# A graph kernel with 6,656 gathers: each gather waits until GpSimd is done with the one ahead

## The chip, the cores and the metric

The kernel runs on one core of one Trainium2 chip. The metric is the device time of one execution in microseconds; the number given for a kernel is the median of its runs.

## What is computed

Two layers of a graph network over 6,250 nodes of 128 features and 206,250 edges (200,000 drawn at random and a loop per node). The first weighs, sums and feeds a small network; the second makes three hops of attention over the edges. Cut to its core:

```python
def _L0_gnn_ref(x, edge_index, edge_weight, W1, b1, W2, b2):
    msg = edge_weight[:, None] * x[src]
    agg = jax.ops.segment_sum(msg, dst, num_segments=N)
    h = jax.nn.relu((x + agg) @ W1 + b1)
    return h @ W2 + b2

def _L1_gnn_ref(entity_emb, edge_emb, q_w, k_w, edge_index, edge_type, ...):
    rel = edge_emb[edge_type]
    for _ in range(3):
        h, t = agg[head], agg[tail]
        att = jnp.sum((h @ q_w) * jnp.tanh(rel * t @ k_w), axis=1)
        w = segment_softmax(att, head)
        agg = segment_sum(w[:, None] * rel * t, head) / max(count, 1)
        agg = agg / norm(agg)
        out = out + agg + entity_emb
    return out

x = _layernorm(x + _L0_gnn_ref(...))
x = _layernorm(x + _L1_gnn_ref(...))
```

What matters here is `x[src]` in the first layer and `agg[tail]` in each hop: a row of 512 bytes, found by an index, for every edge, four times over.

## The kernel before

Edges are sorted by the node that they end in (first layer) or start from (hops), so that each section of 128 nodes owns a run of tiles of 128 edges. There are 1,664 tiles (`slot_tiles`), worked on in 416 groups of four (`GROUP`). The program has four long stages that go over all 416 groups: the first layer, with the second sort woven into it, and hops 0, 1 and 2. Short stages lie ahead, between and behind.

In each long stage one gather fetches the 128 node rows of one tile, one row to a partition. It is an indirect DMA of GpSimd, which alone can issue one: GpSimd makes the descriptors and starts the transfer. `pool_rows` (L616) issues them. A batch is two groups (`BATCH`), eight gathers. The gathered rows go to a ring of four groups (`RING`), two batches; the indices to a buffer of two batches. For a batch GpSimd waits until the rows of the ring are consumed (`s_free`, which is `s_rt`) and until ScalarE has copied the indices (`s_copy_idx`), and then issues eight gathers without any wait between them. Each gather adds 16 to `sp_tail` of its group when its data have landed. The first two batches of a stage are written out, all others are in a loop whose waits are against registers (`freed`, `copied`).

In a hop the others do this with a group, each lagging behind the last by a few groups. SyncE loads the group's type rows (`rel`), its mask and four windows of `qt`. VectorE multiplies the type rows with the gathered rows (`rt<-banks,tails`, L1771) once they have landed, and signals `s_rt`. TensorE turns the product (L1833), multiplies it with `k_sb` (L1829); ScalarE copies (`rtt`, L1853) and takes the tanh (`right`, L1849). TensorE makes the attention (L1818), VectorE its minimum (L1759), ScalarE the exponentials (`weight`, L1866), TensorE turns those (L1825) and sums the tile into its section (L1838), and VectorE adds that to the accumulator (L1753). ScalarE copies a batch's indices with `idx<-tails_of_slots` (`scalar_idx`, L645 to L650; the first two batches in `first_idx`, L641) once `s_rt` says that the indices of the batch before were used. So the loop is: gathers, landing, product on VectorE, index copy on ScalarE, the wait of GpSimd, gathers.

In the first layer VectorE and TensorE do a lighter job of the same shape, and ScalarE weighs the gathered rows (L1394) and signals `s_rt`.

Of the kernel before, what the change touches and what calls it, by code (L numbers as in the profile page):

```python
# [145 lines left out]
def phases(e, name, step, groups, total, rates, unroll=UNROLL):  # L146

    regs = {rate: e.alloc_register(f"{name}_rate{rate}") for rate in rates}
    spare = [e.alloc_register(f"{name}_until{n}") for n in range(8)]
    for start in range(0, total, IN_BLOCK):  # L150
        whole = start + IN_BLOCK <= total
        for i in range(start, start + 2 * unroll if whole else total):
            step(Step(e, i, groups))
        if whole:
            turns = IN_BLOCK // unroll - 2
            for rate in rates:
                e.reg_mov(regs[rate], rate)
            with e.Fori(0, turns) as turn:
                for b in range(unroll):
                    step(Step(e, start + 2 * unroll + b, groups, turn, regs, spare, unroll, turns))  # L160
                for rate in rates:
                    e.reg_add(regs[rate], regs[rate], rate)
    for r in [*regs.values(), *spare]:
        e.free_register(r)


def gnn_two_layers(nc, x, src, dst, edge_type, edge_weight, w1, b1, w2, b2, edge_emb, q_w, k_w, out):
    z = Sizes(x.shape[0], src.shape[0], x.shape[1], edge_emb.shape[0])
    assert z.D == P and z.T * 2 == P and z.groups % UNROLL == 0
    top = ExitStack()  # L170
    with top:
        def sem(name):
            return Sem(top.enter_context(nc.semaphore(name)))

        def tensor(ctx, name, shape, dt=F32):
            return ctx.enter_context(nc.sbuf_tensor(name, shape, dt))
# [25 lines left out]
        s_iota, s_consts = sem("s_iota"), sem("s_consts")  # L202
# [404 lines left out]
        sums = acc_of[:, :, 0:z.D]  # L607
        sp_tail = [sem(f"sp_tail{i}") for i in range(RING)]
        s_copy_idx, s_taken, s_acc, s_rt = sem("s_copy_idx"), sem("s_taken"), sem("s_acc"), sem("s_rt")
        stretches = range(0, z.slot_tiles, BANK)  # L610
        full, odd_rows = divmod(z.N, P)

# [2 lines left out]

        def pool_rows(e, name, rows, idx, of, s_free):  # L616

            def batch(b):
                for t in range(BATCH * GROUP):
                    g = b * BATCH + t // GROUP  # L620
                    e.indirect_dma_start(out=rows[:, g, t % GROUP, :], out_offset=None, in_=of,  # L621
                                         in_offset=bass.IndirectOffsetOnAxis(ap=idx[:, b, t:t + 1], axis=0)).then_inc(sp_tail[g].h, 16)

            for b in range(2):
                e.wait_ge(s_copy_idx.h, s_copy_idx.at(b + 1))
                batch(b)
            freed, copied = e.alloc_register(f"freed_{name}"), e.alloc_register(f"copied_{name}")
            e.reg_mov(freed, s_free.at(BATCH))
            e.reg_mov(copied, s_copy_idx.at(3))
            with e.Fori(0, z.slot_groups // BATCH // 2 - 1):  # L630
                for b in range(2):
                    e.wait_ge(s_free.h, s_free.at(BATCH))
                    e.wait_ge(s_free.h, freed)
                    e.wait_ge(s_copy_idx.h, copied)
                    batch(b)
                    e.reg_add(freed, freed, BATCH)
                    e.reg_add(copied, copied, 1)
            e.free_register(freed)
            e.free_register(copied)

        def first_idx(e, others, idx):  # L641
            for b in range(2):
# [21 lines left out]
        with ExitStack() as ctx:  # L664
# [359 lines left out]
            begun = tensor(ctx, "runs_begun", [H, K, P])  # L1024
# [3 lines left out]
            idx = tensor(inner, "l0_idx", [P, 2, BATCH * GROUP], I32)  # L1028
# [385 lines left out]
            with nc.Block() as block:  # L1414
# [24 lines left out]
                def _(e):  # L1439
                    phases(e, "gt", tensor_l0, z.slot_groups, steps, (UNROLL, GROUP * UNROLL))  # L1440
            inner.close()
            s_copy_idx.base += z.slot_groups // BATCH + 1
            for s in (s_rt, s_acc):
                s.base += z.slot_groups
# [251 lines left out]
        for hop in range(HOPS):  # L1696
            with ExitStack() as ctx:
                qt = tensor(ctx, f"qt{hop}", [P, z.NP])
                idx = tensor(ctx, f"idx{hop}", [P, 2, BATCH * GROUP], I32)
# [242 lines left out]
                def scalar_nodes(e):  # L1942
                    a, b = squares
                    e.wait_ge(s_taken.h, s_taken.at(z.slot_tiles))
                    e.activation(square[:, a:b, :], sums[:, a:b, :], ACT.Square).then_inc(s_root.h, 1)
                    e.activation(square[:, b:, :], sums[:, b:, :], ACT.Square).then_inc(s_root.h, 1)
                    e.wait_ge(s_node.h, s_node.at(10))
                    e.activation(norm[:, :], norm[:, :], ACT.Sqrt).then_inc(s_root.h, 1)
# [3 lines left out]
                with nc.Block() as block:  # L1952
                    @block.sync
                    def _(e):
                        e.wait_ge(s_qt.h, s_qt.at(node_groups))
                        pipeline(e, f"hs{hop}", sync_hop, z.slot_groups, deep, (UNROLL,) if first else (UNROLL, GROUP * UNROLL))
                        if first:
                            for s in s_keep:
                                e.wait_ge(s.h, 32 * z.slot_groups // UNROLL)
                        if hop < HOPS - 1:  # L1960
                            for n, (a, b) in enumerate(zip(thirds, thirds[1:])):
                                e.wait_ge(s_node.h, s_node.at(13 + n))
                                e.dma_start(node_rows.rearrange("(t p) d -> p t d", p=P)[:, a:b, :], agg[:, a:b, :]).then_inc(s_next.h, 16)
                            e.wait_ge(s_next.h, 48 * (hop + 1))

                    @block.gpsimd
                    def _(e):
                        pool_rows(e, f"hop{hop}", tails, idx, node_rows, s_rt)

                    @block.vector  # L1970
                    def _(e):
                        vector_q(e)
                        pipeline(e, f"hd{hop}", vector_hop, z.slot_groups, deep, (UNROLL, 2 * UNROLL, GROUP * UNROLL, 16 * GROUP, 32))
                        vector_nodes(e)

                    @block.tensor
                    def _(e):
                        tensor_q(e)
                        pipeline(e, f"he{hop}", tensor_hop, z.slot_groups, deep, (UNROLL, GROUP * UNROLL, 16 * GROUP))

                    @block.scalar
                    def _(e):
                        first_idx(e, others, idx)
                        scalar_q(e)
                        pipeline(e, f"ha{hop}", scalar_hop, z.slot_groups, deep, (UNROLL, GROUP * UNROLL, 32))
                        scalar_nodes(e)
                s_copy_idx.base += z.slot_groups // BATCH + 1
                for s in (s_oht, s_rel, s_copied) if first else (s_copied,):
                    s.base += z.slot_groups
# [60 lines left out]
```

## Time and profile before

| | us |
|---|---|
| median of three runs | 9158.42 |
| lowest, highest | 9154.59, 9167.25 |
| span of the profiled execution | 14895.7 |
| GpSimd busy in it | 6417.6 |
| TensorE busy in it (matmuls) | 9009.4 |
| VectorE, ScalarE busy in it | 6224.1, 6149.7 |

The profiled execution's own time is known by its span alone. It is 5,737 us longer than the median of the runs that were timed without a profiler. Busy times and counts of instructions are those of the program; waits and idle times are those of the profiled execution, and have to be weighed one by one. The gathers are the rows of line L621. A gather's record covers GpSimd's work on it, not the transfer.

### The profile page before, as it was taken

The numbers are of one execution on the slowest core, as the hardware profiler recorded it, in microseconds if no ns is written. First come the engines' busy times: TensorE is split into PE (matmuls) and PEld (weight loads), VectorE is DVE, ScalarE is ACT, GpSimd is POOL, SyncE is SP. The second block draws the span as 40 slices with busy tenths as digits, with TensorE's granted clock in tenths as the row PEclk, the third lists the DMA queues.
The fourth block names the chain that finished last, engine by engine and source line by source line (L and its number), as shares of the span: only waits on it lengthen the run. The fifth ranks groups of instructions, "written<-read, shape, count | busy, mean of one in ns | idle before, by whom it ended". The sixth has DMA issues, their size and how long they took to land. (4 is left out here: it accounts for less than half of the span.)

```text
span 14895.7 us, 251017 instructions
## 1 busy us (share of the span) xinstructions
PE 9009.4 (60%) x47197; PEld 6806.5 (46%) x47197; DVE 6224.1 (42%) x27880; ACT 6149.7 (41%) x15788; POOL 6417.6 (43%) x6756
## 2 busy tenths in 40 slices
PE   2465555566777777777755555555555556555665
PEld 2343443444555555555544444444444444444444
DVE  3555555565333333333343333333334333333334
ACT  1355555553333333333334444444443444444443
POOL 4554554442444434444334444444434444444443
PEclk7566666667777777777777777777777777777777
DMA  2111111112444444444433333333343333333333
GB/s 63 37 37 34 36 35 35 33 35 77 127 125 126 125 125 126 125 125 126 124 102 105 106 104 106 104 105 101 108 99 105 104 104 107 102 105 105 109 109 93
DMA packets 1390477, 1399.81 MB, mean 94 GB/s; under 512 B 239512, under 2 KB 1066681, under 8 KB 1390137
## 3 DMA queue, kind: packets, MB, share of 16 engines
q1 hardware_dynamic: 1173398, 951.42, 21.2%
q0 software_dynamic: 216064, 444.28, 12.3%
q10 hardware_dynamic: 876, 2.56, 0.1%
q8 instruction: 51, 0.84, 0.0%
q14 instruction: 88, 0.71, 0.0%
HBM read 888.87 MB, written 183.76 MB: 72 GB/s over the span
## 5 line engine op out<-in xcount | busy, mean ns | idle before, releaser
L621 POOL DMA_INDIRECT tails<-node_rows,idx x4992 | 4732.3, 948 | 6564.6 <-ACT idx L649 5017.2
L1753 DVE SCALAR_TENSOR_TENSOR acc<-acc,fade,banks 128x129 f32 x4992 | 1718.4, 344 | 5486.8 <-remote 3164.9
L1838 PE MATMUL banks<-rt,weight_t 128*128 128x129 f32 x9984 | 1783.3, 335 | 1486.3 <-issue 802.1
L1838 PEld LDWEIGHTS banks<-rt,weight_t 128*128 128x128 f32 x9984 | 1607.8, 244 | 1631.4 <-issue 1206.6
L621 POOL DMA_INDIRECT l_rows<-in_x_dram,l_idx x1664 | 1585.1, 953 | 1529.5 <-ACT l_idx L649 1017.3
L1846 ACT ACTIVATE weight_t<-banks 128x512 f32<-128x512 f32 x1248 | 745.5, 597 | 3569.1 <-remote 2286.4
L1825 PE MATMUL banks<-ident,weight 128*128 128x128 f32 x4992 | 1070.4, 353 | 1878.0 <-ACT weight L1866 1767.1
L1818 PE MATMUL banks<-right,window 128*128 128x128 f32 x9984 | 1774.8, 335 | 459.9 <-issue 459.2
L1818 PEld LDWEIGHTS banks<-right,window 128*128 128x128 f32 x9984 | 1590.2, 242 | 538.2 <-issue 510.7
L1829 PE MATMUL banks<-rtt,k_sb 128*128 128x512 f32 x2496 | 1741.3, 789 | 1.4 <-ACT rtt L1853 1.4
L1825 PEld LDWEIGHTS banks<-ident,weight 128*128 128x128 f32 x4992 | 752.0, 181 | 2041.5 <-ACT weight L1866 1931.4
L1759 DVE CUSTOM_DVE_ANT_0 att<-banks,mask 128x128 f32<-128x128 f32 x4992 | 1236.7, 285 | 888.7 <-remote 574.4
L1866 ACT ACTIVATE weight<-att,low 128x128 f32<-128x128 f32 x4992 | 1583.4, 395 | 1.7 <-DVE low L1789 1.5
L1853 ACT ACTIVATE rtt<-banks 128x512 f32<-128x512 f32 x1248 | 743.4, 596 | 1597.2 <-remote 1447.3
L1849 ACT ACTIVATE right<-banks 128x512 f32<-128x512 f32 x1248 | 744.4, 596 | 1535.2 <-remote 798.3
L1833 PEld LDWEIGHTS banks<-ident,rt 128*128 128x128 f32 x4992 | 781.9, 172 | 1247.7 <-issue 894.1
L1771 DVE TENSOR_TENSOR rt<-banks,tails 128x512 f32<-128x512 f32 x1248 | 857.9, 687 | 547.2 <-remote 180.2
L1833 PE MATMUL banks<-ident,rt 128*128 128x128 f32 x4992 | 937.3, 321 | 241.5 <-DVE rt L1771 237.0
L1239 ACT ACTIVATE apart<-spread,spot_left 128x256 f32<-128x256 f32 x1534 | 655.2, 495 | 1030.0 <-remote 761.9
L1406 PE MATMUL banks<-l_weighed,l_hot 128*128 128x128 f32 x3328 | 756.5, 395 | 428.2 <-DVE acc L1371 217.7
L1406 PEld LDWEIGHTS banks<-l_weighed,l_hot 128*128 128x128 f32 x3328 | 649.6, 289 | 559.2 <-issue 549.1
L1394 ACT ACTIVATE l_weighed<-l_rows,l_weights 128x128 f32<-128x128 f32 x1664 | 526.8, 387 | 546.1 <-remote 394.4
(309 smaller groups left out, 9792.2 us busy)
## 6 DMA issues: line engine op xcount, KB each, us to landing
window<-qt SPq DMA_DIRECT2D x4992, 64.0 KB
rel<-rel_kept SPq DMA_DIRECT2D x832, 256.0 KB
rows_in<-tile_rows SPq DMA_DIRECT2D x416, 256.0 KB
rel_kept<-rel SPq DMA_DIRECT2D x416, 256.0 KB
mask<-mask_kept SPq DMA_DIRECT2D x832, 128.0 KB
tails<-node_rows,idx POOLq DMA_INDIRECT x4992
mask_kept<-mask SPq DMA_DIRECT2D x416, 128.0 KB
l_rows<-in_x_dram,l_idx POOLq DMA_INDIRECT x1664
```

Source lines behind the costliest of these rows:

```text
L621: e.indirect_dma_start(out=rows[:, g, t % GROUP, :], out_offset=None, in_=of, in_offset=bass.IndirectOffsetOnAxis(ap=idx[:, b, t:t + 1], a ...
L1406: mm = s.e.matmul(bank[g2][:, t * P:t * P + P], hot[:, g2, t, :], weighed[:, g2, t, :], start=True, stop=True)
L1753: e.scalar_tensor_tensor(to, to, fade[:, g2, t:t + 1], bank[b_acc + t // 2][:, t % 2 * WIDE:t % 2 * WIDE + WIDE], ALU.mult, ALU.add).then_ ...
L1759: e.tensor_tensor_reduce(att[:, g2, t, :], bank[b_att][:, t * P:t * P + P], mask[:, g4, t, :], 1.0, START, ALU.add, ALU.min, tile_low[:, g ...
L1771: e.tensor_tensor(rt[:, g4, :, 0:z.D], of, tails[:, g8, :, :], ALU.mult).then_inc(s_rt.h, 1)
L1818: mm = e.matmul(bank[b_att][:, t * P:t * P + P], window[:, g4, t, :], right[:, g2, t * P:t * P + P], start=True, stop=True)
L1825: mm = e.transpose(bank[b_et][:, t * P:t * P + P], weight[:, g2, t, :], ident[:, :])
L1829: e.matmul(bank[b_kw][:, :], k_sb[:, :], rtt[:, s.slot(2, 2), :], start=True, stop=True).then_inc(s_kw.h, 1)
L1833: mm = e.transpose(bank[b_rtt][:, t * P:t * P + P], rt[:, s.slot(1, UNROLL), t, 0:z.D], ident[:, :])
L1838: mm = e.matmul(bank[b_acc + t // 2][:, t % 2 * WIDE:t % 2 * WIDE + WIDE], weight_t[:, s.slot(4, 2), t, :], rt[:, s.slot(4, UNROLL), t, :] ...
L1846: e.activation(weight_t[:, s.slot(4, 2), :, :].rearrange("p t d -> p (t d)"), bank[b_et][:, :], ACT.Copy).then_inc(s_ets.h, 1)
L1866: e.activation(weight[:, g2, t, :], att[:, g2, t, :], ACT.Exp, scale=-1.0, bias=low[:, g4, t + 1:t + 2]).then_inc(s_exp.h, 1)
```

## The change

A semaphore (`s_iota`, used at the start of the program up to the value 2 and free since) counts the gathers that GpSimd has finished: each gather gets `engine_sem=s_begun.h`, by which GpSimd adds one when its own work on the gather is done, which is not when the data have landed. A register `begun` counts how many have been issued. Each gather but the first of a batch waits until the semaphore has reached the register, that is until the gather ahead is done. The wait against a constant above it is always met by then. At the end of each stage the base of the semaphore moves on by 1,664.

```diff
         s_copy_idx, s_taken, s_acc, s_rt = sem("s_copy_idx"), sem("s_taken"), sem("s_acc"), sem("s_rt")
+        s_begun = s_iota
+        s_begun.base += 2
...
         def pool_rows(e, name, rows, idx, of, s_free):
+
+            begun = e.alloc_register(f"begun_{name}")
+            e.reg_mov(begun, s_begun.at(0))
 
             def batch(b):
                 for t in range(BATCH * GROUP):
                     g = b * BATCH + t // GROUP
+                    if t:
+                        e.wait_ge(s_begun.h, s_begun.at(1))
+                        e.wait_ge(s_begun.h, begun)
                     e.indirect_dma_start(out=rows[:, g, t % GROUP, :], out_offset=None, in_=of,
-                                         in_offset=bass.IndirectOffsetOnAxis(ap=idx[:, b, t:t + 1], axis=0)).then_inc(sp_tail[g].h, 16)
+                                         in_offset=bass.IndirectOffsetOnAxis(ap=idx[:, b, t:t + 1], axis=0), engine_sem=s_begun.h)\
+                        .then_inc(sp_tail[g].h, 16)
+                    e.reg_add(begun, begun, 1)
...
-            e.free_register(freed)
-            e.free_register(copied)
+            for r in (freed, copied, begun):
+                e.free_register(r)
...
             s_copy_idx.base += z.slot_groups // BATCH + 1
+            s_begun.base += z.slot_tiles
...
```

The order of the other engines' instructions is the same before and after. On GpSimd, the end of hop 0's written-out batches and its loop before:

```order
L621 DMA tails<-node_rows,idx 128x128 x16
L630 UNCONDITIONAL_BRANCH
L621 DMA tails<-node_rows,idx 128x128 x8
L636 ISA
L621 DMA tails<-node_rows,idx 128x128 x8
L636 ISA
L630 COMPARE_AND_BRANCH
```

And the second batch of that loop now, with the semaphores that a row waits for (`s_iota` is the one that counts finished gathers):

```order
L629 DMA tails<-node_rows,idx 128x128 [waits s_copy_idx,s_rt]
L632 REGISTER_ALU
L629 DMA tails<-node_rows,idx 128x128 [waits s_iota]
L632 REGISTER_ALU
L629 DMA tails<-node_rows,idx 128x128 [waits s_iota]
L632 REGISTER_ALU
L629 DMA tails<-node_rows,idx 128x128 [waits s_iota]
```

Eight gathers that followed each other with nothing between now have a register instruction behind each (the last one's is merged with those that end the batch) and a wait ahead of each but the first. The wait against the register is an instruction of its own in the built program, and the one against the constant is carried by the gather.

## Rows read from the trace of the kernel before

**Rows 1.** The page: span, and part 1, busy us of each engine
```profile
span 14895.7 us, 251017 instructions
PE 9009.4 (60%) x47197; PEld 6806.5 (46%) x47197; DVE 6224.1 (42%) x27880; ACT 6149.7 (41%) x15788; POOL 6417.6 (43%) x6756
```

**Rows 2.** Line L621: durations min/median/max ns; what ended idle time: us, times
```profile
L621 POOL DMA_INDIRECT tails<-node_rows,idx x4992: 939/946/1395, 3532.0 to 14810.8; - x200
L621 POOL DMA_INDIRECT l_rows<-in_x_dram,l_idx x1664: 939/946/1212, 160.5 to 3251.3; - x185
...
  ACT idx L649: 5017.2, 618
  issue: 1900.0, 5891
```

**Rows 3.** Timeline of POOL, one batch in hop 1: start us, us, what, idle
```profile
9009.08 0.96 POOL L621 DMA_INDIRECT tails<-node_rows,idx  x1 [7.24 <-ACT idx L649]
...
9017.84 0.94 POOL L621 DMA_INDIRECT tails<-node_rows,idx  x1 [0.30 <-issue]
9025.32 0.95 POOL L621 DMA_INDIRECT tails<-node_rows,idx  x1 [6.54 <-ACT idx L649]
```

**Rows 4.** Windows: length; busy of PE, PEld, DVE, ACT, POOL; clock, DMA share, GB/s
```profile
9009.00:9013.00 4.00, 3.42 (x26) 2.70 (x25) 3.09 (x17) 2.76 (x8) 3.01 (x4) 1.00 0.37 99
9013.00:9018.60 5.60, 1.26 (x12) 1.07 (x10) 0.00 (x0) 0.00 (x0) 4.38 (x5) 0.94 0.47 141
9018.60:9025.30 6.70, 4.30 (x16) 3.16 (x17) 3.18 (x17) 4.25 (x12) 0.19 (x1) 0.54 0.21 61
```

**Rows 5.** Timeline of ACT around the same batch
```profile
9018.67 0.60 ACT L1853 ACTIVATE rtt<-banks 128x512 f32<-128x512 f32 x1 [5.97 <-remote]
...
9024.35 0.20 ACT L649 ACTIVATE idx<-tails_of_slots 128x8 int32 x1
```

**Rows 6.** Timeline of PE, one group there
```profile
9007.99 1.06 PE L1838 MATMUL banks<-rt,weight_t 128*128 128x129 f32 x8
9008.88 1.06 PE L1818 MATMUL banks<-right,window 128*128 128x128 f32 x8
9010.52 0.66 PE L1825 MATMUL banks<-ident,weight 128*128 128x128 f32 x4 [0.58 <-ACT weight L1866]
9011.01 1.02 PE L1829 MATMUL banks<-rtt,k_sb 128*128 128x512 f32 x2
9011.88 0.60 PE L1833 MATMUL banks<-ident,rt 128*128 128x128 f32 x4
```

**Rows 7.** Timeline of POOL where long stages end and begin
```profile
3251.30 0.95 POOL L621 DMA_INDIRECT l_rows<-in_x_dram,l_idx  x1 [0.30 <-issue]
...
3531.97 0.95 POOL L621 DMA_INDIRECT tails<-node_rows,idx  x1 [17.11 <-ACT idx L643]
...
7435.71 0.94 POOL L621 DMA_INDIRECT tails<-node_rows,idx  x1 [0.31 <-issue]
...
7498.83 0.98 POOL L621 DMA_INDIRECT tails<-node_rows,idx  x1 [62.17 <-ACT idx L643]
...
11145.83 0.95 POOL L621 DMA_INDIRECT tails<-node_rows,idx  x1 [0.30 <-issue]
...
11204.25 0.95 POOL L621 DMA_INDIRECT tails<-node_rows,idx  x1 [57.48 <-ACT idx L643]
...
14810.78 0.94 POOL L621 DMA_INDIRECT tails<-node_rows,idx  x1 [0.30 <-issue]
```

**Rows 8.** Lines L634 and L636, POOL's sequencer: durations min/median/max ns; first and last start
```profile
L634 POOLq EVENT_SEMAPHORE  x824: 42/43/43, 173.3 to 14801.3; - x165
...
L636 POOLq FUSED_REGOPS  x824: 42/51/54, 177.2 to 14805.0; - x165
```

**Rows 9.** Timeline of ACT and of POOL, the first gather of the program
```profile
160.03 0.31 ACT L643 ACTIVATE l_idx<-l_others 128x8 int32<-128x8 int32 x2
...
160.51 0.95 POOL L621 DMA_INDIRECT l_rows<-in_x_dram,l_idx  x1 [22.85 <-ACT l_idx L643]
```

More of the change, by code:

```diff
@@ L1986, in _ @@
                         scalar_nodes(e)
+                s_begun.base += z.slot_tiles
                 s_copy_idx.base += z.slot_groups // BATCH + 1
```

## The prediction

> **What bounds the kernel now.** I read the page's first lines first: the profiled execution spans 14895.7 us, the median of the undisturbed runs is 9158.42 us, and no engine is busy for more than 60% of the span [rows 1]. The profiled execution is therefore not a picture of the timed one, and durations may be carried over only where something shows that they hold. So I went to GpSimd's own rows. A gather's record is 946 ns long in the median, in all 6,656 of them, and the gap to the next one is 0.30 us, 5,891 times, with nothing named that it waits for [rows 2]. In the timeline of one batch of eight the first gather begins at 9009.08 and the last at 9017.84: seven periods of 1.251 us. Then GpSimd is idle for 6.54 us until ScalarE has copied the next indices [rows 3].
>
> That idle time is where the profiled execution departs. While GpSimd has gathers left, the other engines stop: from 9013.0 to 9018.6 VectorE and ScalarE start nothing, against 3.09 and 2.76 busy us in the 4 us ahead [rows 4]. ScalarE's copy of rtt starts 5.97 us late, at 9018.67, by a release that no instruction of the program explains, and only then do the two groups go on that free the next batch [rows 5]. Left alone, the others are faster than that: TensorE's five pieces of one group take 1.06, 1.06, 0.66, 1.02 and 0.60 us at the full clock (the window of rows 4 shows 1.00), 4.4 us, and ran within 4.5 us, from 9007.99 to 9012.48 [rows 6]. A group has four gathers, 4 x 1.251 = 5.0 us. **Undisturbed, GpSimd would be the slowest engine.**
>
> The median can be tested against that. Time without gathers, from the places where a stage ends and the next begins [rows 7]: 160.5 us ahead of the first gather, 3531.97 - 3251.30 - 1.25 = 279.4, 7498.83 - 7435.71 - 1.25 = 61.9, 11204.25 - 11145.83 - 1.25 = 57.2, and 14895.7 - 14810.78 - 1.25 = 83.7 at the end; 643 us in all. Gathers back to back: 6,656 x 1.251 = 8,327 us. Together 8,970 us, 188 us (2%) under the median. A stall of 5.6 us in each of 832 batches can't be in 9158 us: its sum alone is 4,659 us, and with 8.8 us of TensorE's work per batch it would make 14.4 us, where the median leaves (9158 - 643) / 832 = 10.2. So I take it that the stall belongs to the profiled execution, and that the timed one is a chain of gathers.
>
> **The change, part by part.** No instruction of the other engines is moved. On GpSimd each gather adds one to a semaphore when the engine is done with it, which costs nothing that a row shows. A register is added to after each gather; that runs in the sequencer, whose such instructions take 51 ns [rows 8], and lies beside the gather that runs. Each gather but the first of a batch of eight gets a wait: 7 x 832 = 5,824 waits. The one against the register stands as an instruction of its own ahead of the gather, so the sequencer can't hand the gather over before the one ahead is done. Before the change it could: from the wait that opens a batch (first and last of these at 173.3 and 14801.3) to the register instruction behind the eighth gather (177.2 and 14805.0) are 3.7 to 3.9 us, so a hand-over takes some 0.46 to 0.49 us, and eight are through while GpSimd works off three [rows 8]. That preparation is now bare, seven times in a batch.
>
> What does such a restart cost? The nearest row is the start of a batch, which has the same form (a wait against registers as its own instruction, then a gather): the index copy ends at 9024.35 + 0.20 = 9024.55 and the gather begins at 9025.32, 0.77 later [rows 3, 5]. I take 0.77 in place of 0.30, that is 0.47 us more. The end of GpSimd's own instruction may be told sooner or later than the end of its record, and the wait's form may matter, so both ends:
> - from below, the first gather of the program, whose only wait is a constant that the gather itself carries: the two index copies begin at 160.03, the first ends some 0.20 later, and the gather begins at 160.51, some 0.28 later [rows 9]. Then nothing is lost, and 0.02 us per gather, 120 us in all, is even gained;
> - from above, completion told only at the moment at which the next gather could begin today, 0.30 after the record's end, and then the whole restart: 1.07, that is 0.77 more, 4,484 us.
>
> The sum is 5,824 x 0.47 = 2,737 us, on the path, since GpSimd sets it. The first gather of a batch stays covered: its waits are looked at while the eighth runs for 0.95 us. Behind the waiting gather stand only other gathers and the index waits; VectorE's product with the tails waits for their landing, then the index copy of ScalarE for the product. That loop has 13.3 us per batch (8 x 1.251 + 7 x 0.47) where it had 10.0, so it has more room, not less. Against this kernel's own parts: 8,970 + 2,737 = 11,707. The 188 us that the floor lacks are either others' work that now disappears behind GpSimd, or remain: 11,895. I take the middle, **11,800 us**. Made against the profiled span the sum would be another: its idle time on GpSimd (5017.2 us until the index copies of the hops alone [rows 2]) could take up all 2,737, and would stay so if the stalls stay.
>
> The record's end might not be the instruction's end. The Trainium skill, "Perfetto Trace Analysis", section "DMA Instruction — SWDGE (GPSIMD)", puts the profiler's end at the last descriptor written, with the end of the instruction itself behind it. By that rule the wait ends later than I take and the sum leans toward its upper end; no row here separates the two moments.
>
> A second rule speaks against the change. A gather's record never begins before the last one's has ended, by 0.30 us throughout [rows 2, 3]. The Trainium skill, "GPSIMD Engine Reference", section "Instruction dispatch", says that a core of GpSimd starts on the next instruction as soon as its own share of the last is finished, without regard to the other cores. By that, queued gathers may overlap inside the 0.30 us and the wait would take that away as well, which again is the upper end of 13,450; the rows show no overlap of the records.
>
> **The rivals.**
> - *The hand-over is hidden.* The sequencer prepares the gather although the wait ahead of it isn't met, or completion is told early. For it: the 0.28 us of the first gather. Against it: the 0.77 of the batch start, whose form the added waits have. It gives 9,040 us and, with gaps up to 0.34, 9,400.
> - *A dearer restart.* Completion told late, 1.07 us between gathers, 13,450 to 13,640 us; or TensorE, idle for a third of the time, is granted the lower clock (in rows 4 it stands at 1.00 in the busy stretch and at 0.54, near the 1.2 GHz level, behind the pause), at which two groups take up to 17.6 us of matmul, over the 13.3 us of GpSimd.
> - *Faster.* Gathers that stand in GpSimd's queue are what stops the other engines [rows 4, 5], and this is so without a profiler, in part. Then a batch of 10.2 us is not GpSimd's but theirs, and holding gathers back sets them free at 8.8 us per batch. GpSimd would need 8 x 0.946 + 7 x 0.28 + 0.30 = 9.8 us, 643 + 832 x 9.83 = 8,820 us. It decides only if the gap with the wait is below (10.23 - 7.57 - 0.30) / 7 = 0.34 us. For it: the stall is plain in the trace and ends as the last queued gather starts. Against it: the floor of 8,970, and 0.77.
> - *The others hid it anyway.* They would have to need 13.3 us per batch; the median leaves 10.2. I give it nothing.
>
> **How the numbers follow.** Forecast 0.74; hidden hand-over 0.09 (of which 0.02 faster, 0.03 within 0.2%, 0.04 slower); dearer 0.10; faster by the queue 0.07. A measurement of this kernel can tell about 0.2%, 18 us, from no change. So faster 0.09, same 0.03, slower 0.88. Within the forecast the hand-over outside the profiler may be quicker than 0.46 us: at 0.3 the loss is 0.31 us each, 643 + 8,327 + 1,805 = 10,775. The range is 10,800 to 13,600, from there to the late completion; left out are the faster and the hidden cases and the lower clock, under 2 in 10.
>
> **What the profile after would show.** Gaps between gathers of a batch near 0.77 us, released by GpSimd itself, seven of eight; a first gather of a batch that still follows at 0.30 wherever the indices are early; records of 946 ns as before. If the stalls hang on queued gathers they go, and the profiled span falls to some 11,700 to 12,100 us although the timed runs get slower; if they stay, it is up to 17,600. Gaps of 0.3 us would make me wrong, as would timed runs below 9,400. Gaps of 0.77 with a time near 9,158 would mean that GpSimd never was the bound.

## The result, and the profile after

The changed kernel takes 11,733.07 us (median of 4 runs, 11,730.14 to 11,737.47) against 9,162.83 us (9,154.59 to 9,172.63) for the kernel before, beside it on the same chip: **1.2805 times, 95% interval 1.2787 to 1.2823**, 2,570 us slower. The forecast was 11,800 us. Three later measurements gave 1.2812, 1.2801 and 1.2806.

The page of the changed kernel: its span and part 1 (busy us of each engine), and of part 5 the gathers and VectorE's product. They answer to [rows 1, 2]:

```profile
span 11732.5 us, 262673 instructions
...
PE 8072.8 (69%) x47197; PEld 6039.7 (51%) x47197; DVE 6250.6 (53%) x27880; ACT 6294.0 (54%) x15788; POOL 6404.6 (55%) x6756
...
L629 POOL DMA_INDIRECT tails<-node_rows,idx x4992 | 4712.0, 944 | 3706.3 <-DMA tails<-node_rows,idx 3230.4
...
L1782 DVE TENSOR_TENSOR rt<-banks,tails 128x512 f32<-128x512 f32 x1248 | 862.9, 691 | 2707.5 <-DMA tails<-node_rows,idx 2624.9
```

The span fell from 14,895.7 to 11,732.5 us, while the timed runs rose from 9,163 to 11,733. GpSimd's gathers still cost 944 ns each; what ends its idle time has changed. The same line's durations (min/median/max ns) and what ended its idle time (us, times):

```profile
L629 POOL DMA_INDIRECT tails<-node_rows,idx x4992: 938/942/1455, 3252.0 to 11651.9; - x200
L629 POOL DMA_INDIRECT l_rows<-in_x_dram,l_idx x1664: 938/943/1203, 165.2 to 2982.2; - x185
...
  DMA tails<-node_rows,idx: 3230.4, 4319
  DMA l_rows<-in_x_dram,l_idx: 1110.2, 1441
  issue: 450.2, 885
...
  ACT idx L659: 11.5, 3
```

The releaser named "DMA tails" is the gather ahead, whose semaphore the added wait looks at. 4,319 + 1,441 = 5,760 gaps lie behind such a wait, and they last 3230.4 / 4,319 = 0.748 us in the hops and 1110.2 / 1,441 = 0.770 us in the first layer. Before, a gap was 0.30 us. The wait for ScalarE's index copy, 5,017.2 us in [rows 2], is 11.5 us; most of that fall isn't the change's, as the experiments show (140.3 us in three_ahead, which is as fast as the kernel before). VectorE now waits 2,624.9 us for gathered rows.

One batch in hop 0, from GpSimd's timeline (start us, us, what, idle time and what ended it), which answers to [rows 3]:

```profile
4997.01 0.95 POOL L629 DMA_INDIRECT tails<-node_rows,idx  x1 [0.31 <-issue]
5001.24 0.94 POOL L629 DMA_INDIRECT tails<-node_rows,idx  x1 [3.28 <-issue]
5002.94 0.94 POOL L629 DMA_INDIRECT tails<-node_rows,idx  x1 [0.76 <-DMA tails<-node_rows,idx]
5004.63 0.94 POOL L629 DMA_INDIRECT tails<-node_rows,idx  x1 [0.75 <-DMA tails<-node_rows,idx]
...
5011.49 0.94 POOL L629 DMA_INDIRECT tails<-node_rows,idx  x1 [0.75 <-DMA tails<-node_rows,idx]
5012.74 0.94 POOL L629 DMA_INDIRECT tails<-node_rows,idx  x1 [0.31 <-issue]
```

The first gather of a batch follows at 0.31 us, the others at 0.75: a period of 1.69 us for 1.25. And there is something that the prediction doesn't have: a gap of 3.28 us (3.30 in the first layer), ahead of the second gather of a batch. It comes every 104 gathers (13 batches), 15 times in each stage and 60 times in the program.

What GpSimd's sequencer does in the 0.75 us, from the starts of the three kinds of row behind the gather that begins at 5001.24 and ends at 5002.18 (waits L628, gathers L629, register instructions L632, in the window from 5002 to 5005):

```profile
L628 POOLq EVENT_SEMAPHORE  x2: 17/17/17, 5002.2 to 5003.9; - x2
...
L632 POOLq ALU_OP  x2: 32/32/32, 5002.7 to 5004.4; - x2
```

The wait passes at 5002.2, at once after the end of the gather ahead. The register instruction that stands behind the new gather runs at 5002.7, so the sequencer needed 0.5 us to hand the gather over, and the gather begins at 5002.94. Gather, wait, hand-over, gather: nothing overlaps any more. In the long gap it is the same with a longer hand-over: the wait passes at 4997.99, the register instruction runs at 5001.02, 3.03 us later.

The four long stages (length; busy of PE, PEld, DVE, ACT, POOL; clock, DMA share, GB/s):

```profile
167.00:2983.00 2816.00, 1738.73 (x10197) 1307.63 (x10197) 1673.86 (x4865) 1544.54 (x3612) 1593.93 (x1663) 0.56 0.16 40
3252.00:6021.00 2769.00, 2350.48 (x14104) 1686.17 (x14103) 1523.79 (x7842) 1495.27 (x3933) 1572.67 (x1664) 0.92 0.62 177
6075.00:8838.00 2763.00, 1880.39 (x10799) 1439.12 (x10798) 1336.73 (x7025) 1530.98 (x3938) 1569.33 (x1664) 0.90 0.50 138
8890.00:11653.00 2763.00, 1873.03 (x10797) 1437.58 (x10796) 1327.92 (x7025) 1525.68 (x3936) 1569.97 (x1664) 0.91 0.50 138
```

All three hops are now of one length, though hop 0 has 470 us more of TensorE's work than hop 1. That is what a chain of gathers looks like.

### The profile page after: what moved, and what is told of

It is laid out like the page before. It is cut to its first block and busy times, and to the rows that moved or that the text cites. A ratio compares the mean times of both kernels' runs of the same rounds, so it can differ in the third digit from the quotient of the medians.

```text
span 11732.5 us, 262673 instructions
## 1 busy us (share of the span) xinstructions
PE 8072.8 (69%) x47197; PEld 6039.7 (51%) x47197; DVE 6250.6 (53%) x27880; ACT 6294.0 (54%) x15788; POOL 6404.6 (55%) x6756
## 5 line engine op out<-in xcount | busy, mean ns | idle before, releaser
L629 POOL DMA_INDIRECT tails<-node_rows,idx x4992 | 4712.0, 944 | 3706.3 <-DMA tails<-node_rows,idx 3230.4
L1849 PE MATMUL banks<-rt,weight_t 128*128 128x129 f32 x9984 | 1600.1, 309 | 1077.2 <-DVE acc L1764 1072.7
L1782 DVE TENSOR_TENSOR rt<-banks,tails 128x512 f32<-128x512 f32 x1248 | 862.9, 691 | 2707.5 <-DMA tails<-node_rows,idx 2624.9
L629 POOL DMA_INDIRECT l_rows<-in_x_dram,l_idx x1664 | 1595.0, 959 | 1246.9 <-DMA l_rows<-in_x_dram,l_idx 1110.2
L1849 PEld LDWEIGHTS banks<-rt,weight_t 128*128 128x128 f32 x9984 | 1375.1, 213 | 1324.2 <-issue 1312.0
L1844 PEld LDWEIGHTS banks<-ident,rt 128*128 128x128 f32 x4992 | 568.3, 145 | 2079.7 <-DVE rt L1782 1909.7
L1829 PE MATMUL banks<-right,window 128*128 128x128 f32 x9984 | 1614.9, 314 | 0.6 <-DVE tile_low L1770 0.5
L1844 PE MATMUL banks<-ident,rt 128*128 128x128 f32 x4992 | 819.5, 288 | 1092.9 <-DVE rt L1782 1085.2
L1829 PEld LDWEIGHTS banks<-right,window 128*128 128x128 f32 x9984 | 1463.3, 225 | 31.8 <-ACT right L1860 0.9
L1840 PE MATMUL banks<-rtt,k_sb 128*128 128x512 f32 x2496 | 1369.7, 632 | 1.4 <-ACT rtt L1864 1.4
L1836 PE MATMUL banks<-ident,weight 128*128 128x128 f32 x4992 | 849.6, 298 | 32.2 <-ACT weight L1877 31.9
L1264 PE MATMUL banks<-in_column,paid 128*64 128x256 f16 x3328 | 707.6, 386 | 197.5 <-ACT in_column L1253 128.2
L1384 DVE SCALAR_TENSOR_TENSOR l_hot<-banks,l_low_of 128x512 f32<-128x512 f32 x416 | 287.5, 691 | 957.1 <-PE banks L1416 956.7
```

Source lines behind the costliest of these rows:

```text
L1782: e.tensor_tensor(rt[:, g4, :, 0:z.D], of, tails[:, g8, :, :], ALU.mult).then_inc(s_rt.h, 1)
L1829: mm = e.matmul(bank[b_att][:, t * P:t * P + P], window[:, g4, t, :], right[:, g2, t * P:t * P + P], start=True, stop=True)
L1836: mm = e.transpose(bank[b_et][:, t * P:t * P + P], weight[:, g2, t, :], ident[:, :])
L1840: e.matmul(bank[b_kw][:, :], k_sb[:, :], rtt[:, s.slot(2, 2), :], start=True, stop=True).then_inc(s_kw.h, 1)
L1844: mm = e.transpose(bank[b_rtt][:, t * P:t * P + P], rt[:, s.slot(1, UNROLL), t, 0:z.D], ident[:, :])
L1849: mm = e.matmul(bank[b_acc + t // 2][:, t % 2 * WIDE:t % 2 * WIDE + WIDE], weight_t[:, s.slot(4, 2), t, :], rt[:, s.slot(4, UNROLL), t, :] ...
```

## The experiments

Twelve measurements were made, on three chips, and every ratio below is against the kernel before, measured beside it on the same chip. On one chip the kernel before takes 14,894.42 us (14,815.88 to 14,940.92, 14 runs); below, this is "the stalling chip". On the two others it takes 9,171.48 on one, 9,165.59 and 9,162.16 on the other.

### One part of the change alone, and fewer waits, on the stalling chip

*Counting without waiting.* The semaphore and the register stay, both waits go:

```diff
-                    if t:
-                        e.wait_ge(s_begun.h, s_begun.at(1))
-                        e.wait_ge(s_begun.h, begun)
```

> The semaphore increment and the register additions of the change stay, all 5,824 waits are gone. Theory (the cost is the restart of GpSimd behind each wait): gap between gathers 0.30 us again, time that of before, 9,160 us within 20, and the profiled execution shows the stalls of before again, span some 14,900 us. Rival (counting itself costs, the completion semaphore slows each gather): the time stays well above 9,160 us; at half of the added 2,570 it would be 10,440. Of the profiled execution: if the stalls are gone here too, it is the semaphore and not the empty queue that ends them.

Measured: 14,875.4 us, ratio 0.9992 (0.9967 to 1.0017). The count and the register instructions cost nothing here. (Here the chain of gathers isn't the bound; that they are free where it is, three_ahead shows below.) But the number itself was a surprise: this is the length of the profiled execution of [rows 1], in timed runs, and the kernel before takes 14,894 us beside it. From this run's page, the span and the gathers (busy us, mean ns, idle us, what ended most of it):

```profile
span 14872.7 us, 251017 instructions
...
L626 POOL DMA_INDIRECT tails<-node_rows,idx x4992 | 4734.2, 948 | 6538.3 <-ACT idx L656 4991.8
```

4,991.8 us of waiting for the index copy, as in [rows 2]. So **the stall of [rows 4, 5] isn't the profiler's doing**. It goes with the chip: the kernel before is that slow in all 14 runs on this one and in none of the 33 on the two others. Whether this chip always stalls is not known, since its runs were all made one after the other.

*Waiting for the gather two ahead.* At most one gather then is queued behind the one that runs:

```diff
-            e.reg_mov(begun, s_begun.at(0))
+            e.reg_mov(begun, s_begun.at(-1))
...
-                    if t:
+                    if t >= 2:
```

> As the change, but a gather waits for the one two ahead of it, not for its neighbour; the same kind of wait, 6 of them in a batch of 8 in place of 7. Theory: the hand-over of the next gather (0.5 us) now lies beside the one that runs (0.95 us), so the gap falls back to about 0.30 us and the time to 9,160 to 9,250 us. Rival (each wait costs by itself, some 0.45 us, whatever it waits for): 6 x 832 x 0.44 = 2,200 us more than before, 11,360 us. Profiled execution: at most one gather is queued behind the running one; if a deep queue is what stops the other engines, the span falls near the timed value here too, some 9,300 us.

Measured: 14,995.04 us, ratio 1.0068 (1.0045 to 1.0091). The gaps stay at 0.30 us and the stall stays as well. GpSimd's timeline and ScalarE's around the end of a batch:

```profile
9012.11 0.94 POOL L629 DMA_INDIRECT tails<-node_rows,idx  x1 [0.31 <-issue]
9020.92 0.94 POOL L629 DMA_INDIRECT tails<-node_rows,idx  x1 [7.87 <-ACT idx L659]
```

```profile
9006.38 0.60 ACT L1860 ACTIVATE right<-banks 128x512 f32<-128x512 f32 x1 [0.26 <-PE banks L1840]
9014.27 0.60 ACT L1864 ACTIVATE rtt<-banks 128x512 f32<-128x512 f32 x1 [7.29 <-remote]
```

ScalarE starts nothing for 7.29 us and is then released by nothing that the program explains, as in [rows 5]. So a queue of one gather doesn't prevent the stall. Nor does the stall end with the queue: the last gather of the batch begins at 9012.11 and ends at 9013.05, and ScalarE goes on 1.22 us after that. VectorE goes on later still: in hop 1, 2.2 us after the end of the last gather in the median batch.

*One wait per batch,* the middle one, 832 in all:

```diff
-                    if t:
+                    if t == 4:
```

> As the change, with the wait ahead of the fifth gather of a batch alone: 832 waits in place of 5,824. Theory (0.44 us per restart, on GpSimd's chain): 832 x 0.44 = 370 us over before, 9,530 us. Rival (the others, not GpSimd, are the bound of before, and only a longer batch shows): a batch of 10.0 + 0.45 = 10.45 us against 10.2 hides most of it, time 9,160 to 9,300 us. Profiled execution: up to four gathers queued; between 9,530 and 14,900 us, the nearer to the first the more the stall hangs on a queue of more than four.

Measured: 14,704.89 us, ratio 0.9891 (0.9848 to 0.9934), a little faster where the chain of gathers isn't the bound. It prices no wait here; below it is measured where nothing stalls. But it tells something of the stall. GpSimd's timeline at the waiting gather of one batch, and VectorE's behind it:

```profile
9017.19 0.95 POOL L629 DMA_INDIRECT tails<-node_rows,idx  x1 [0.75 <-issue]
```

```profile
9023.63 0.35 DVE L1764 SCALAR_TENSOR_TENSOR acc<-acc,fade,banks 128x129 f32 x1 [7.58 <-remote]
```

VectorE is idle from 9016.05 to 9023.63. From 9016.44 to 9017.19 no gather runs or is queued, since the fifth waits until the fourth is done. VectorE isn't released by that; it goes on 1.74 us after the batch's last gather has ended at 9021.89. In hops 1 and 2 it is idle across this pause, for over 2.5 us, in 189 of 208 batches each; where nothing stalls, the same kernel has one such batch per hop. So a pause of 0.75 us without any gather, which is what the change has between its gathers, doesn't end a stall.

*Half of the gathers.* Of the kernel before, every second gather is left out, their rows in the ring stay zero, and those who wait for landed rows wait for half the count; half of the graph's edges don't count:

```diff
-                for t in range(BATCH * GROUP):
+                for t in range(0, BATCH * GROUP, 2):
```

> The kernel before with every second gather of both layers left out (four per batch in place of eight); the rows not gathered are zeros, so the sums lack those edges, and all other engines do the same work. Theory (GpSimd's chain is the bound of before at 1.251 us per gather): its chain halves to 4,164 us and the others become the bound at 4.4 to 5.5 us per group, 643 + 1,664 x 5 = 8,900 us at most and 643 + 1,664 x 4.4 = 7,960 us at least. Rival (the others are the bound of before at 10.2 us per batch): no change, 9,160 us. If stalls by queued gathers were there without a profiler, the relief would be larger than the theory's.

Measured: 10,617.97 us, ratio 0.7132 (0.7111 to 0.7154). Per batch that is (14,894 - 10,618) / 832 = 5.1 us for four gathers fewer, about their own 4 x 1.25 = 5.0: with fewer gathers the stall is shorter. It can't be told from this run how fast the others would be alone, since 10,618 holds stalls too; the other chips tell it below.

### The change and its price on the other chips

*The change once more,* unaltered.

> The change itself, beside new runs of the kernel before (14,894 us beside the last four kernels, where 9,158 was measured ahead of the prediction). Theory: with the change no gather is ever queued behind a running one, so whatever stops the other engines in the profiled execution of before and in its later timed runs can't act; the time is 11,733 us again, within 20, whatever the kernel before does: 0.79 of it if before takes 14,890 us, 1.28 if it takes 9,160. Rival (the chip of these runs is slower as a whole): the change is slower too, by the 1.63 of before or a part of it, over 12,500 us.

Measured: 11,746.78 us against 9,171.48, ratio 1.2812 (1.2791 to 1.2833); the span is 11,745.8. Every run of these experiments has its span on record, and on each chip the spans of the kernel before lie about 2 us under its times. The profiler lengthens nothing.

*The loop written out, with constant waits.* The register waits stand apart from the gather; does it matter? Here batches and waits are written out, so that each wait is against a constant and is carried by the gather itself, and no register instruction is left:

```diff
+            for n in range(z.slot_groups // BATCH):
...
                     if t:
...
+                        e.wait_ge(s_begun.h, s_begun.at(n * BATCH * GROUP + t))
```

> As the change, each gather but the first of a batch waits for its neighbour, but GpSimd's loop is written out, so the values are constants and the gather carries the wait itself; no instruction stands between two gathers of a batch. Theory (the change costs the hand-over of a gather, 0.5 us, which a wait as an instruction of its own lays bare): the hand-over goes on beside the running gather, gap 0.28 to 0.33 us, 5,824 x 0.45 = 2,600 us less than the change: 9,000 to 9,350 us, if a gather that waits for a semaphore doesn't count as queued; if it does, the stalls are back and it is 14,900 where before is. Rival (completion is told late and each wait costs 0.45 us by itself): gap 0.75, 11,730 us.

Measured: 9,233.3 us, ratio 1.007 (1.0053 to 1.0087). The order is as strict as in the change, each gather waits for the one ahead, and 2,500 of the 2,570 us are gone. GpSimd's timeline of one batch in it:

```profile
5504.51 0.94 POOL L628 DMA_INDIRECT tails<-node_rows,idx  x1 [0.30 <-DMA tails<-node_rows,idx]
...
5508.25 0.94 POOL L628 DMA_INDIRECT tails<-node_rows,idx  x1 [0.31 <-DMA tails<-node_rows,idx]
5509.50 0.94 POOL L628 DMA_INDIRECT tails<-node_rows,idx  x1 [0.30 <-issue]
```

The gaps behind a wait are 0.30 us, those of a gather without one. So completion is told early enough to start the next gather where it starts anyway, and **the price of the change is the hand-over alone**. It is paid only where the wait is an instruction of its own, ahead of the gather. The Trainium skill, "Perfetto Trace Analysis", section "DMA Instruction — SWDGE (GPSIMD)", describes the queue that this takes: the sequencer pushes the instruction into a wait queue and goes on to the next, and the semaphore is waited for in that queue. By that, a carried wait comes behind the push and costs none of it, and this trace agrees, with 0.30 us carried and 0.75 us apart.

*The same without waits,* to see what the form of the loop does:

```diff
-                    if t:
-                        e.wait_ge(s_begun.h, s_begun.at(n * BATCH * GROUP + t))
```

> The control for the written-out loop: the same code without the waits between gathers. Theory: as the kernel before beside it, within 1% (14,890 us in the last runs). Rival (writing the loop out costs or saves by itself, by the fetching of 6,656 instructions): another time; what const_waits gives has then to be read against this one.

Measured: 9,177.02 us, ratio 1.0005 (0.9995 to 1.0014). The form does nothing; the 56 us between these two are the waits'. They go back to the rare long hand-over: in const_waits 15 gaps of 1.72 us stand in the first layer and as many in hops 1 and 2, at the places where the change has 3.28 to 3.30 and the kernel without waits 0.30. That is 45 x 1.41 = 64 us. In hop 0 both have gaps of 2.04 us there, and both take 2,219 us.

*Waiting for the gather three ahead,* five waits per batch against the register, each an instruction of its own as in the change:

```diff
-            e.reg_mov(begun, s_begun.at(0))
+            e.reg_mov(begun, s_begun.at(-2))
...
-                    if t:
+                    if t >= 3:
```

> As the change, but a gather waits for the one three ahead of it, so up to two are queued behind the running one. Waiting two ahead gave 14,995 us and all the stalls of before. Theory (one queued gather is enough for a stall): within 200 us of the kernel before beside it, 14,900 us in the last runs. Rival (the stalls of the two-ahead kernel come from its waits): at 5 waits a batch in place of 6 the time falls below both, 14,700 us or less.

Measured: 9,169.92 us, ratio 1.000 (0.999 to 1.001). 4,160 waits of the same kind as the change's, with the same count and register instructions, and they cost nothing, since the hand-over lies beside two gathers. It is not the number of waits that costs. No trace of the kernel before itself was kept from these two chips, so this one serves as the picture of it, undisturbed; its time is the same, and flat_no_waits has the same stages within 3 us. The page's span and part 1, and the four stages with the columns of the table above.

```profile
span 9164.4 us, 259345 instructions
...
PE 7129.8 (78%) x47197; PEld 5381.7 (59%) x47197; DVE 6309.0 (69%) x27880; ACT 6171.5 (67%) x15788; POOL 6403.2 (70%) x6756
```

```profile
169.00:2263.00 2094.00, 1434.81 (x10170) 1110.30 (x10170) 1656.08 (x4846) 1536.87 (x3593) 1587.24 (x1664) 0.74 0.22 53
2543.00:4762.00 2219.00, 2165.97 (x14049) 1584.11 (x14048) 1593.34 (x7811) 1437.32 (x3914) 1574.37 (x1664) 0.99 0.78 220
4823.00:6911.00 2088.00, 1636.40 (x10762) 1248.41 (x10762) 1330.03 (x7008) 1487.86 (x3918) 1570.74 (x1664) 0.99 0.66 182
6981.00:9068.00 2087.00, 1636.82 (x10756) 1248.65 (x10755) 1321.85 (x7006) 1485.34 (x3918) 1569.83 (x1664) 0.99 0.66 182
```

Three of the stages are 2,087 to 2,094 us long, 1,664 gathers at 1.255 to 1.26: a chain of gathers. In hop 0 TensorE is busy for 2,166 of 2,219 us at a granted clock of 0.99. That stage is TensorE's.

### One wait per batch and half of the gathers again, where nothing stalls

*The change a third time,* as the upper mark. It was meant for the stalling chip too and met another.

> So far the kernel before took 9,171 us in all 19 runs on one chip and 14,894 us in all 14 on another; the change was run on the first alone, 11,747 us. Theory (on some chips a gather that is queued behind a running one stops the other engines; the change queues none): 11,730 to 11,750 us on either kind of chip. On one where before takes 14,890 that is a ratio of 0.79, and the profile is free of pauses in which VectorE and ScalarE start nothing. Rival (such a chip is slow for every kernel of this make): over 12,500 us there. Where before takes 9,170 us this run says nothing new.

Measured: 11,730.12 us against 9,165.59, ratio 1.2801 (1.278 to 1.2823).

*One wait per batch again,* the same kernel as above.

> The kernel with the wait ahead of the fifth gather of a batch alone, 832 waits, which took 14,705 us where before took 14,894. On a chip where before takes 9,170: theory (a restart costs 0.444 us on GpSimd's chain, which is the bound but in hop 0, where TensorE is busy 98% of the time and paces it at 1.33 us per gather): 624 x 0.444 = 277 us outside hop 0 and little in it, where 8 x 1.251 + 0.44 = 10.45 us is below TensorE's 10.67; 9,440 to 9,460 us. Rival (the price falls on every batch): 832 x 0.444 = 369 us, 9,540. Rival (others are the bound everywhere): under 9,200 us. On a chip where before takes 14,890: 14,705 us again, since gathers are still queued.

Measured: 9,448.14 us (9,444.59 to 9,460.32), ratio 1.0311 (1.0294 to 1.0328), which is 283 us more than before. GpSimd's idle time ahead of its gathers (us, times; `issue` in all stages, the waits on the gather ahead in the three hops), and the wait in the timeline:

```profile
  issue: 1702.0, 5506
  DMA tails<-node_rows,idx: 466.4, 624
```

```profile
5507.60 0.94 POOL L629 DMA_INDIRECT tails<-node_rows,idx  x1 [0.30 <-issue]
5509.29 0.94 POOL L629 DMA_INDIRECT tails<-node_rows,idx  x1 [0.75 <-DMA tails<-node_rows,idx]
5510.54 0.94 POOL L629 DMA_INDIRECT tails<-node_rows,idx  x1 [0.30 <-issue]
```

A bare hand-over costs 0.45 us. 832 of them would be 374 us; the 624 outside hop 0 are 281, and 283 were measured. Hop 0 grew by 4.5 us only, against three_ahead, because there TensorE is the bound and hides GpSimd's loss.

*Half of the gathers again,* with the same half left out.

> The kernel with every second gather of both layers left out, which took 10,618 us where before took 14,894. On a chip where before takes 9,170: theory (outside hop 0 GpSimd's chain is the bound of before, TensorE in hop 0): hop 0 stays at 5.33 us per group, hops 1 and 2 fall from 5.02 to the others' own pace, at least TensorE's 4.4 and likely 4.6 to 4.9, the first layer from 5.03 to 4.3 to 4.9; 643 + 416 x (5.33 + 3 x 4.7) = 8,730 us, at least 8,350 and at most 9,050. Rival (others are the bound everywhere): 9,170 us.

Measured: 8,402.89 us (8,397.37 to 8,408.37) against 9,162.16, ratio 0.9173 (0.9158 to 0.9188). Two stretches of it, one in hop 0 and one in hop 1, with the columns of the tables above:

```profile
2300.00:4400.00 2100.00, 2060.00 (x13338) 1505.29 (x13339) 1497.31 (x7417) 1362.90 (x3717) 745.80 (x789) 0.99 0.65 196
4500.00:6400.00 1900.00, 1584.83 (x10906) 1272.70 (x10904) 1340.17 (x7114) 1468.80 (x3963) 782.74 (x830) 0.99 0.62 175
```

With GpSimd idle for more than half of the time, the program gains only 759 us: the other engines' own pace is no slower than 8,403 us, and hop 0 is at it already. On the stalling chip the same kernel took 10,618, so 2,215 us of stalls were in that, against 5,729 with all gathers.

*The change a fourth time,* also meant for the stalling chip.

> The change once more, for a chip where the kernel before takes 14,890 us, on which it hasn't run yet. Theory: 11,730 to 11,750 us there too, a ratio of 0.79. Rival (such a chip is slow for every kernel of this make): over 12,500 us. Where before takes 9,170 us this run says nothing new: 1.28.

Measured: 11,734.25 us, ratio 1.2806 (1.2785 to 1.2828), again not on the stalling chip. What the change does there was never measured.

## Why the prediction was right, point by point

**The bound: right.** Undisturbed, the kernel before is a chain of gathers at 1.25 us in three of its four stages, and removing gathers shortens it (0.9173).

**The stall: the observation right, the step "the stall belongs to the profiled execution" wrong.** The reasoning was that 5.6 us in 832 batches can't be in 9,158 us, which is so, and from that it took the profiler for the cause. Timed runs on one chip show the same 14,894 us. The profiled execution of the kernel before has the length that this chip gives; that it was taken on such a chip is the plain reading, though nothing records where it was. The reading that the stall ends as the last queued gather starts doesn't hold either: in the two-ahead kernel ScalarE goes on 1.22 us after that gather's end. The consequence drawn was the same, since the numbers were to be compared with the median. But the range of the text should then have asked "on which chip". If it is queued gathers that stall, the change would be faster there: by its own chain it would take about 11,730 us against 14,894. That isn't shown. Neither the change nor a carried wait was run on the stalling chip, and two traces speak against it: the stall outlasts the queue (e2_two_ahead) and goes on where the queue is empty for 0.75 us (e3_one_wait).

**The hand-over: right in mechanism, a little too dear.** 0.77 us was taken in place of 0.30. The first layer has 0.770, the hops 0.748; the mean over all is (3230.4 + 1110.2) / 5,760 = 0.754, which is 0.449 more than the 0.305 of three_ahead's gaps (1,313.5 us in 4,310). The other two parts of the step were the ends: "from below", the first gather's carried constant, is what const_waits shows, but for another form of wait; "from above", completion told late, fell with it, and so did the lean toward the upper end that the rule on the record's end gave. Those two readings of the nearest row were both true, each of its own form, and the order of the built instructions had decided which applied. The overlap inside the 0.30 us that the prediction held possible is worth nothing: where every gather but the first waits for the one ahead (const_waits), the gaps stay at 0.30.

**The sum.** From the starts of the first and last gather of each stage, three_ahead against the change: 2,094 to 2,817, 2,218 to 2,768, 2,087 to 2,761 and 2,087 to 2,762 us. The 2,568 us between the spans, 9,164.4 and 11,732.5, come apart thus:

| | us |
|---|---|
| 5,760 bare hand-overs at 0.449 | +2,586 |
| 60 long hand-overs, 3.29 in place of 0.30 | +179 |
| hop 0: TensorE's pace, 2,218 - 2,087, no longer the bound | -131 |
| ahead of, between and behind the stages, 679 to 625 | -54 |
| what is left (a gap of 9.4 to 9.5 us at the start of hops 1 and 2, 2.5 to 2.6 in the change; records 3 us longer in all) | -12 |

The term of the prediction was 2,737. It was 151 us too high for the hand-overs (5,824 x 0.47), and didn't hold the 179 of the long ones. The two errors hide each other: the sum came out well by luck in this.

**The missing 188 us: located.** The prediction took half of them as others' work that disappears and half as something that stays. They are 131 us of TensorE's pace in hop 0, and the rest small things at stage edges. The larger part disappeared, so the floor of 11,707 was the better of the two figures; the middle, 11,800, is 67 us above the result. What the trace before could have told was that hop 0 has more TensorE work than the others; [rows 6] priced a group in hop 1, and that price was put on all stages.

**The first gather of a batch stays covered: right,** at 0.31 us. **Records stay as they were: right,** 942 and 943 ns for 946.

**The dearer rival: half seen, and worth nothing.** TensorE is granted less: 0.90 to 0.92 in the hops where three_ahead has 0.99, and 0.56 in the first layer for 0.74. It costs no time because TensorE isn't the bound. In hop 0, the heaviest, it is busy for 2,350 of 2,769 us, and the hop is as long as the other two. **The faster rival** needs a stall in the timed runs and a gap under 0.34. Neither was so on the chips where the change was timed. **The hidden hand-over** exists, in another form of the same order: const_waits at 1.007 is what that rival priced at 9,040 to 9,400.

**The profiled span** came out at 11,732.5, in the 11,700 to 12,100 named for the case that the stall hangs on queued gathers. The later spans of the change, 11,724 to 11,746, come from chips where nothing stalls with queued gathers either, so this is no proof of it.

## What to carry to other kernels

Ask of a wait whether the instruction carries it or whether it stands apart, and what the sequencer has left to do behind it: on GpSimd a gather's hand-over takes 0.5 us, free beside a gather that runs and wholly on the path behind a wait of its own, 0.45 us each, 5,760 times. If the order must be kept, wait for the gather three ahead (1.000) or write the waits out against constants (1.007 for the strict order); where nothing stalls, none of the versions that compute the whole beats the kernel before. And when a profiled execution and the timed runs differ by half, don't put it down to the profiler: here timed runs on another chip have the profiled length.

## What the runs showed of the hardware that was not expected

- **On one of three chips the other engines stop while a batch of gathers is worked off.** The kernel before takes 14,894 us on it and 9,162 to 9,171 on the other two, 1.62 times. With a queue of one gather instead of seven the time is as long (e2_two_ahead, 14,995); whether gathers that are never queued do it too wasn't tried. VectorE goes on some 2.2 us after a batch's last gather has ended. The loss grows with the number of gathers: 5,729 us with 6,656, 2,215 us with 3,328. Even GpSimd's own register instructions are caught: in the two-ahead kernel they take up to 709 ns there, and 45 at most in three_ahead on another chip. The transfers themselves aren't slower: by part 3 of the pages, the packets of the two large DMA queues took 33.7% of 14,872.7 us in e1_count_only and 56.0% of 9,164.4 in three_ahead, some 5,010 and 5,130 us. What in the chip does it stays open.

The register instructions of the two kernels (min/median/max ns), first the two-ahead kernel on the stalling chip, then three_ahead:

```profile
L632 POOLq ALU_OP  x4996: 5/32/709, 164.6 to 14987.5; - x200
```

```profile
L632 POOLq ALU_OP  x4164: 32/32/45, 168.5 to 9064.0; - x199
```

- **Every 104th gather has a hand-over of some 3.0 us in place of 0.5.** The gap is 3.28 to 3.30 us where the hand-over is bare (15 per stage, the change), 1.72 us where one gather can be handed over ahead (const_waits), and can't be found in the first layer of three_ahead, where all 1,663 gaps are below 0.31 us. So it hides beside two gathers. In hop 0 of three_ahead, where GpSimd waits for the others, it shows: 15 gaps of 1.9 to 2.05 us at the same places. It goes by the gathers and not by time or by the form of the loop: the places are the same in the change (175 us apart in the first layer), in const_waits (131 us apart, loop written out) and in hop 0 of three_ahead, and the count begins anew in each stage, with the first at its 114th gather. With four gathers in a batch (half_again) they come every 108 gathers. What recurs wasn't found.
- **A gather's completion costs no time of its own.** With the wait carried, the next record begins 0.30 us after the last, as if no wait were there.
